# Flamingo layer on one core: TensorE takes over additions of tile 12 and of three outputs, and the slots are reordered

## What is computed

```python
x = x + tanh(g_xattn[0]) * xattn(layernorm(x), ctx, ctx, Wq, Wk, Wv, Wo)   # 16 heads of 64, causal
x = x + tanh(g_ffn[0]) * ffn(layernorm(x), ...)

def ffn(x, ...):
    h = rmsnorm(x, gamma1)
    q = (h @ Wq + bq).reshape(b, t, 16, 8)
    kv = ((h @ Wdown + bdown) @ Wup + bup).reshape(b, t, 16, 16)
    k, v = split(kv)
    att = softmax(einsum('bthd,btgd->bthg', q, k) / sqrt(8))       # heads of one row attend to each other
    x = x + einsum('bthg,btgd->bthd', att, v).reshape(b, t, 128) @ Wo + bo
    h2 = rmsnorm(x, gamma2)
    gate = softmax(h2 @ Wg + bg)                                   # 8 experts
    return x + einsum('btd,edf,bte->btf', h2, We, gate)
```

## Time and profile before

| | us |
|---|---|
| median of 3 runs | 265.44 |
| lowest, highest | 265.3, 267.71 |
| the profiled execution | 265.66 |
| its span | 263.8 |
| PE, DVE, ACT, POOL busy | 236.0, 195.0, 168.3, 159.0 |

### The profile page before, as it was taken

One profiled execution on the slowest core, in us unless ns is written; L12 is line 12 of the kernel. 1 busy time (PEld: TensorE's weight loads), 2 busy tenths in 40 slices (PEclk: granted clock), 3 DMA queues, 4 the chain that ended last, 5 costly groups with the idle time before them and its releaser, 6 DMA issues.

```text
span 263.8 us, 7717 instructions
## 1 busy us (share of the span) xinstructions
PE 236.0 (89%) x3154; PEld 167.0 (63%) x3154; DVE 195.0 (74%) x335; ACT 168.3 (64%) x498; POOL 159.0 (60%) x169
## 2 busy tenths in 40 slices
PE   5989989898999999998999999989999988851781
PEld 3765778586768585857676776867685665530360
DVE  0236644198989796979798832989897999999925
ACT  2437634756686868785877778667868767651452
POOL 4104041619196877878587376691968778739644
PEclk9999999999999999999999999999999999995698
DMA  6990000000000000000000000000000000000000
GB/s 212 369 307 6 2 4 0 6 0 2 0 5 10 2 14 0 4 10 5 11 2 12 2 10 4 10 5 0 2 12 2 11 4 14 0 0 0 12 10 20
DMA packets 6016, 7.28 MB, mean 28 GB/s; under 512 B 477, under 2 KB 4830, under 8 KB 5982
## 3 DMA queue, kind: packets, MB, share of 16 engines
q1 hardware_dynamic: 5550, 6.16, 7.2%
q10 hardware_dynamic: 432, 0.64, 0.7%
HBM read 5.88 MB, written 0.92 MB: 26 GB/s over the span
## 4 chain that ended last, share of the span: by engine, by line
PE 77%; ACT 9%; DVE 7%; issue 3%; DMA 1%; POOL 0%; SPq 0%; DVEq 0%; ACTq 0%; POOLq 0%
PE ps_a L825 47%; PE ps_c L825 11%; PE ps_b L825 9%; PE ps_e L825 5%; PE ps_b L877 3%; ACT exb L462 2%; DVE ps_e L616 2%; DMA cT<-in_ctx_t 1%; ACT probs L407 1%; ACT probsT L414 1%; ACT v_sb L396 1%; DVE psums L583 1%; PE ps_c L921 1%; DVE exb L684 1%; ACT aT L401 1%
## 5 line engine op out<-in xcount | busy, mean ns | idle before, releaser
L268 POOL TENSOR_TENSOR probs<-probs,prinv 120x672 f32<-120x672 f32 x16 | 24.3, 1517 | 48.3 <-DVE prinv L587 48.2
L277 POOL TENSOR_TENSOR prod<-fqkv 128x1280 f32<-128x1280 f32 (+1 forms) x14 | 38.5, 2752 | 1.9 <-DVE fqkv L601 0.7
L825 PE MATMUL ps_a<-aT,wo_sb 128*128 128x112 f32 x256 | 32.9, 281 | 2.1 <-ACT aT L401 1.3
L825 PEld LDWEIGHTS ps_a<-aT,wo_sb 128*128 128x128 f32 x256 | 29.9, 191 | 4.2 <-ACT aT L401 2.0
L644 DVE TENSOR_REDUCE ps_e<-prod 128x128 f32<-128x2048 f32 x14 | 31.9, 2281 | 0.4 <-POOL prod L288 0.4
L616 DVE TENSOR_REDUCE ps_e<-prod 128x256 f32<-128x2048 f32 x14 | 32.0, 2284 | 0.0
L825 PE MATMUL ps_a<-wv_sb,cT 128*64 128x512 f32 x128 | 31.4, 606 | 0.0
L825 PE MATMUL ps_a<-cT,wk_sb 128*128 128x224 f32 x128 | 28.9, 379 | 1.3 <-DMA cT<-in_ctx_t 1.3
L401 ACT COPY aT<-ps_a 128x448 f32<-128x448 f32 x32 | 15.5, 536 | 20.4 <-PE ps_a L825 20.4
L825 PEld LDWEIGHTS ps_a<-cT,wk_sb 128*128 128x128 f32 x128 | 24.6, 203 | 5.6 <-DMA cT<-in_ctx_t 2.9
L825 PE MATMUL ps_a<-xT,wqc 128*128 128x224 f32 x128 | 27.0, 359 | 0.6 <-ACT qT L390 0.6
(11 more groups left out here) (136 smaller groups left out, 468.9 us busy)
## 6 DMA issues: line engine op xcount, KB each, us to landing
xp_sb<-in_xp SPq DMA_DIRECT2D x1, 896.0 KB, 7.8
out<-out_sb SPq DMA_DIRECT2D x14, 64.0 KB, 1.5
xT<-in_x_t SPq DMA_DIRECT2D x1, 784.0 KB, 9.1
cT<-in_ctx_t SPq DMA_DIRECT2D x1, 784.0 KB, 10.6
wv_sb<-in_wv SPq DMA_DIRECT2D x1, 512.0 KB, 7.7
...
```

The lines of the kernel that those rows point to most:

```text
L268: nc.gpsimd.tensor_tensor(pr[0:TG, NC:C, :, 0:S], pr[0:TG, NC:C, :, 0:S], prinv[p % 2][0:TG, NC:C, :].unsqueeze(3).to_broadcast([TG, C - N ...
L277: nc.gpsimd.tensor_tensor(prod1[:, 0:hp, :, :], t[:, D:2 * D].rearrange("p (g d) -> p g d", g=FH).unsqueeze(1).to_broadcast([128, hp, FH, ...
L825: return nc.tensor.matmul(o, lhsT, rhs, start=start, stop=stop, skip_group_check=True)
```

## The change

For tile 12 (PE_SUMS) the products are written with the summed index outermost (prod1 as d, h, g; prod2 as g, h, d), and TensorE adds them: logit_sums with 8 matmuls of 256 columns and head_sums with 16 of 128, the identity as weights, accumulated in ps_e. For the tiles 10, 11 and 12 (PE_OUT) output_sums adds the ten terms with ten matmuls of 128 columns instead of GpSimd's outputs; ScalarE's late_out copies the sum, and SyncE waits for that copy. Tile 13's exponentiated gate lies in PSUM. stay_warm is gone. In the main loop (steps 2 to 13) TensorE does first(fa) behind turn_probs and gate_logits, shift before bias_o, and attend before both expert halves; ScalarE does x1_copy behind turned_probs; GpSimd does weighted before first_scale; VectorE does weighted before gate_logits and scaled_qkv behind head_sums. Steps 14 and 15 and the part after the loop are reordered on all engines.

```diff
 LATE = 10
 HP_LATE = 8
 HQ_LATE = 5
+PE_SUMS = (12,)
+PE_OUT = (10, 11, 12)
 BIG = {11: "b", 12: "a", 13: "b"}
-STAY_WARM = 10
 PROJECT_AT = {t: [("qk"[t % 2], t // 2 + 1, n) for n in range(4)] for t in range(2, NP - 2)}
 
...
 
         def expert_banks(f):
             return {"a": ps_a, "b": ps_b}[BIG[f]] if f in BIG else ps_c
+
+        prod1_d = prod1[:, :, :, :].rearrange("p a b c -> p (a b c)").rearrange("p (d h g) -> p d h g", d=FD, h=FH)
+        prod2_g = prod2[:, :, :, :].rearrange("p a b c -> p (a b c)").rearrange("p (g h d) -> p g h d", g=FH, h=FH)
...
+
+        def logit_products(f, lo, hi, k, q):
+            if f in PE_SUMS:
+                return (prod1_d[:, :, lo:hi, :],
+                        k.rearrange("p (g d) -> p d g", g=FH).unsqueeze(2).to_broadcast([128, FD, n, FH]),
+                        q.rearrange("p (h d) -> p d h", h=n).unsqueeze(3).to_broadcast([128, FD, n, FH]))
+            return (prod1[:, lo:hi, :, :],
+                    k.rearrange("p (g d) -> p g d", g=FH).unsqueeze(1).to_broadcast([128, n, FH, FD]),
+                    q.rearrange("p (h d) -> p h d", h=n).unsqueeze(2).to_broadcast([128, n, FH, FD]))
+
+        def head_products(f, lo, hi, v):
+            n = hi - lo
+            if f in PE_SUMS:
+                return (prod2_g[:, :, lo:hi, :],
+                        e_sb[f % 2][:, lo:hi, :].rearrange("p h g -> p g h").unsqueeze(3).to_broadcast([128, FH, n, FD]),
+                        v.rearrange("p (d g) -> p g d", d=FD).unsqueeze(2).to_broadcast([128, FH, n, FD]))
+            return (prod2[:, lo:hi, :, :],
+                    e_sb[f % 2][:, lo:hi, :].unsqueeze(2).to_broadcast([128, n, FD, FH]),
+                    v.rearrange("p (d g) -> p d g", d=FD).unsqueeze(1).to_broadcast([128, n, FD, FH]))
+
+        def gate_exp(f):
+            return ps_c[:, 1, 256 + E:256 + 2 * E] if f == NT - 1 else gexp[f % 2][:, :]
+
+        def out_sum(f):
+            return ps_a[:, 1, 0:D] if f == PE_OUT[0] else ps_e[:, 0, 0:D]
 
...
             for f in range(NT):
                 if f == NT - 1:
                     sp.wait_ge(s["last_out"], 1)
+                elif f in PE_OUT:
+                    sp.wait_ge(s["late_out"], f - PE_OUT[0] + 1)
                 else:
                     sp.wait_ge(s["out_ready"], f + 1)
                 sp.dma_start(out[f * 128:(f + 1) * 128, :], out_sb[f % 2][:, :]).then_inc(stored[f % 2], 16)
...
+                o, k, q = logit_products(f, 0, hp, t[:, D:2 * D], t[:, 0:hp * FD])
+                nc.gpsimd.tensor_tensor(o, k, q, ALU.mult).then_inc(s["prod1_pool"], 1)
...
+                o, e, v = head_products(f, 0, hq, fqkv[f % 2][:, 2 * D:3 * D])
+                nc.gpsimd.tensor_tensor(o, e, v, ALU.mult).then_inc(s["prod2_pool"], 1)
...
                 if fc is not None:
                     second_scale(fc)
+                if fb is not None:
+                    weighted(fb)
                 if fa is not None:
                     first_scale(fa)
-                if fb is not None:
-                    weighted(fb)
                 if fc is not None:
                     gating(fc)
...
             last, prior, third = NT - 1, NT - 2, NT - 3
             products(prior)
             first_scale(last)
+            products(last)
             weighted(prior)
-            products(last)
             second_scale(third)
-            outputs(third - 1)
+            weighted(last)
             gating(third)
-            weighted(last)
             second_scale(prior)
-            outputs(third)
+            last_residual(last)
             gating(prior)
             second_scale(last)
-            last_residual(last)
-            outputs(prior)
...
-                nc.scalar.activation(gexp[f % 2][:, :], glog[f % 2][:, :], ACT.Exp, bias=gmax[f % 2][:, :],
+                nc.scalar.activation(gate_exp(f), glog[f % 2][:, :], ACT.Exp, bias=gmax[f % 2][:, :],
                                      accum_out=gsum[f % 2][:, :]).then_inc(s["gexp_ready"], 1)
...
+
+            def late_out(f):
+                act.wait_ge(s["out_summed"], f - PE_OUT[0] + 1)
+                act.wait_ge(stored[f % 2], 16 * (f // 2))
+                nc.scalar.copy(out_sb[f % 2][:, :], out_sum(f)).then_inc(s["late_out"], 1)
...
@@ -499,23 +527,24 @@
                 if fc is not None:
                     squares(fc)
                     x2_copy(fc)
-                if fa is not None:
-                    x1_copy(fa)
                 if fb is not None:
                     head_exps(fb)
                 if t < NP:
                     values(t, 0)
                     values(t, 1)
                     turned_probs(t)
+                if fa is not None:
+                    x1_copy(fa)
                 if fc is not None:
                     gate_exps(fc)
                 if t < NP:
                     attended(t, 0)
                     attended(t, 1)
+                if fc is not None:
+                    experts(fc, 0)
                 if fa is not None:
                     kv_copy(fa)
                 if fc is not None:
-                    experts(fc, 0)
                     experts(fc, 1)
...
                 x2_copy(fc)
+                values(t, 0)
                 squares(fc)
                 x1_copy(fa)
+                values(t, 1)
                 turned_probs(t)
-                values(t, 0)
+                gate_exps(fc)
                 head_exps(fb)
-                values(t, 1)
-                gate_exps(fc)
                 attended(t, 0)
                 attended(t, 1)
                 kv_copy(fa)
...
             last, prior, third = NT - 1, NT - 2, NT - 3
+            x1_copy(last)
             o_copy(third)
-            x1_copy(last)
             head_exps(prior)
+            kv_copy(last)
+            squares(third)
             x2_copy(third)
-            squares(third)
-            kv_copy(last)
+            head_exps(last)
+            late_out(PE_OUT[0])
+            o_copy(prior)
             gate_exps(third)
-            o_copy(prior)
-            head_exps(last)
+            x2_copy(prior)
             squares(prior)
             experts(third, 1)
+            o_copy(last)
             experts(third, 0)
-            x2_copy(prior)
             gate_exps(prior)
-            o_copy(last)
+            squares(last)
+            x2_copy(last)
             experts(prior, 1)
-            x2_copy(last)
-            squares(last)
             experts(prior, 0)
             gate_exps(last)
+            late_out(third)
             experts(last, 0)
+            late_out(prior)
...
+                o, k, q = logit_products(f, hp, FH, ps_e[:, f % 2, 2 * D:3 * D], fqkv[f % 2][:, hp * FD:D])
+                if f - 1 in PE_SUMS:
+                    dve.wait_ge(s["logit_ready"], f)
+                nc.vector.tensor_tensor(o, k, q, ALU.mult).then_inc(s["prod1_ready"], 1)
...
+                if f - 1 in PE_SUMS:
+                    dve.wait_ge(s["oraw_ready"], f)
+                o, e, v = head_products(f, hq, FH, ps_e[:, f % 2, 3 * D:4 * D])
+                nc.vector.tensor_tensor(o, e, v, ALU.mult).then_inc(s["prod2_ready"], 1)
...
-                nc.vector.tensor_scalar(gate[f % 2][:, :], gexp[f % 2][:, :], ginv[f % 2][:, :], r2[f % 2][:, :],
+                nc.vector.tensor_scalar(gate[f % 2][:, :], gate_exp(f), ginv[f % 2][:, :], r2[f % 2][:, :],
                                         ALU.mult, ALU.mult).then_inc(s["gate_ready"], 1)
...
@@ -755,17 +785,17 @@
                     norm(t)
                 if fb is not None:
                     shifted_logits(fb)
+                    weighted(fb)
                 if fc is not None:
                     gate_logits(fc)
                 if fb is not None:
-                    weighted(fb)
-                    head_scales(fb)
+                    head_sums(fb)
                 if fc is not None:
                     gate_sum(fc)
                 if fa is not None:
                     scaled_qkv(fa)
                 if fb is not None:
-                    head_sums(fb)
+                    head_scales(fb)
                     normed_heads(fb)
...
+                gate_sum(fc)
                 weighted(fb)
                 head_scales(fb)
-                gate_sum(fc)
                 head_sums(fb)
...
             last, prior, third = NT - 1, NT - 2, NT - 3
+            new_x1(NP - 1)
             products(prior)
-            new_x1(NP - 1)
-            logits(prior)
+            scaled_qkv(last)
+            shifted_logits(prior)
             new_x2(third)
-            shifted_logits(prior)
-            scaled_qkv(last)
             weighted(prior)
             products(last)
-            head_sums(prior)
             head_scales(prior)
+            logits(last)
+            shifted_logits(last)
             gate_logits(third)
             normed_heads(prior)
-            logits(last)
+            weighted(last)
+            new_x2(prior)
+            head_scales(last)
             gate_sum(third)
```

(92 more changed lines are left out.)

24 lines of the change are left out of this document (3 added, 21 removed).

## The result

Each kernel ran 20 times. The changed kernel took 264.75 us in the median (264.07 to 265.78), the kernel before 266.40 us (264.72 to 268.81): a ratio of 0.995 with a 95% interval of 0.9931 to 0.9969. The forecast was 266.2 us and 0.3% slower. Ratios leave out runs that are over 1.5% longer than the fastest of the same kernel, medians don't, so a ratio can differ a little from that of two medians. Two things stand out. The median of three runs from which the forecast started (265.44) was 1 us better than the median of twenty. And the runs of before spread over 4.1 us, those of after over 1.7.

What follows compares the result with a forecast made beforehand. TensorE bounds the loop (77% of the span), VectorE and then a latency chain the tail. Loop +1.85, steps 14 and 15 +0.1, tail -1.2 give +0.75 on 265.66 us, as a median 266.2 us; range 262.3 to 268.8.

Steps and rivals of the forecast that it cites:

- the loop chain: Steps 2 to 13: with first late, turn_probs of steps 4 and 12 wait for GpSimd's norm; 1.85 us lost in total.
- Full steps: Attention loop: the chain takes 13.9 us where TensorE needs 14.16, so they stay unchanged, margin 0.25 us.
- rival B: Loop: the 13.9 us chain also binds full steps, seven paying 0.3 us each: +2.1, 268.3 us; chance 0.16.
- Rival A: Loop chain slack, waits of steps 2, 3 and 11 gone, last DMA not delayed: 262.5 us; chance 0.28.
- The tail: After the loop: 3 us won at x2, half given back by sums and ScalarE's queue; -1.2 us, bounds -3 to 0.
- The delay by the DMA in front: Last output on SyncE: output_sums(12)'s DMA goes first, the last tile's follows 0.47 us behind, at 260.6.
- Steps 14 and 15: VectorE bounds them and its order hardly changes, one gate_sum of 0.1 us moved ahead: +0.1 us.
- The baseline: Whole kernel: +0.75 on the profiled 265.66 us gives 266.4; the median lies 0.22 below, so 266.2 us.
- rival C: TensorE's clock: logit_sums runs at the low level after idling from 231.0 to 232.3: +3.5, 269.7 us; chance 0.08.
- Those named for being right: TensorE idle before turn_probs(4)/(12) ~1 us; steps 5-8 14.2 us; VectorE idle 2-3 us; clock 1.00; gate below 0.3 us.
- sign of being wrong: scores(13) no later than 189.7 us, or the last tile's x2 over 4 us earlier, counted from scores(13).
- The rule that was weighed: GpSimd's strided products: reads with a step over 8 bytes cost about half again; no extra taken, else tail -0.9.

Runs made afterwards that it cites:

- tail_only: The changed kernel with the old order in steps 2 to 13: 263.56 us, ratio 0.9912 to the kernel before.
- no_warm: The kernel before with stay_warm taken out and nothing else: 265.38 us, ratio 0.9933.
- warm_hole: The kernel before with 40 unread identity matmuls in TensorE's hole from 237 to 243 us: 268.81 us, ratio 1.0089.
- before_again: The kernel before, unchanged, run and profiled once more: 266.84 us, ratio 1.0032 to itself.
- dve_sums: The changed kernel with both sums of tile 12 back on VectorE: 266.94 us, ratio 1.0018 to the kernel before.
- mixed: The changed kernel with the new order only in steps 4 to 8, 12 and 13: 263.05 us, ratio 0.9864 to the kernel before.
- best1: The changed kernel with the old loop order, tile 11's output back on GpSimd, gate_exps before expert terms: 262.66 us, ratio 0.9839 to the kernel before.
- best2: As best1, with the new order in steps 5 to 8 and 13: 262.21 us, ratio 0.9816 to the kernel before.

## Why the prediction was wrong

**The loop: mechanism right, size 0.8 us off.** The prediction had the loop chain late at turn_probs of steps 4 and 12, and it is, released by GpSimd's norm, 0.78 and 0.77 us. Up to scores(5) it had 1.2 us lost; the profiles show 1.64 (start to start from scores(2): 40.51 against 38.87), since already step 3 waits, 1.53 us, where the prediction left turn_probs(3) at 60.65; counted from scores(2) it is at 61.05. For steps 11 and 12 it had 0.65, and they show 0.66. Full steps were to be unchanged with a margin of 0.25 us, and none waits: rival B, that the chain binds in all of them, is out. Rival A, a slack chain, is out by the same waits. Two terms were missing. Step 9 lost 0.52, mostly a wait of 0.56 us for the turned probabilities, which ScalarE handed over late. And in the profile of before steps 6 and 8 were 1.17 us longer than in tail_only, the same order without those issue gaps (14.74 and 15.05 against 14.46 and 14.16), and step 2 was 0.27 shorter: 165.05 against 164.15 us from scores(2) to scores(14). In all six profiles with the new order in steps 5 to 8 these take 14.10 to 14.12 us. So the loop cost 1.07 us in the profiles (166.12 against 165.05) where 1.85 was forecast (the prediction's own two times for scores(13) differ by 1.82); against a loop without gaps it cost 1.97. The long steps stood in the trace of before, and I took one step of 14.16 us for all. Why the gaps come and go isn't settled: of eight profiles with the old order in the full steps, five have them at the same two places, and tail_only, no_warm and warm_hole don't.

**The tail: 1.2 us forecast, 2.3 measured. This is the term that turned the sign in the profiles.** All in times less 1.82 us. VectorE's part came out nearly as laid out: new_x1(15) done at 231.8 (forecast 232.2), heads of tile 13 at 249.98 (250.5), x2 at 251.60 (251.85), sums of 3.72 and 3.81 us (3.5 and 3.7). The step that failed comes behind x2, at output_sums(11) in front of gate_logits(13). The sums were put behind turn_x2 at 252.75 and were to end at 255.4, with the gate's logits at 255.95. Measured, turn_x2 was followed by the sums at 252.02, TensorE was free of them for gate_logits at 254.25, and the logits were done at 254.80, 1.15 us early. The lead lasted to the end: the last output was put at 260.05 and ended at 259.08, where it had been 261.75 before. The delay by the DMA in front, put at 0.5 us, was 0.35. So the span ends 2.3 us earlier than before, where 1.2 was forecast.

**Steps 14 and 15.** Forecast +0.1; step 14 took 0.17 us more (12.13 against 11.96).

**The start.** scores(2) began 0.58 us later in after (39.35 against 38.77), before the first moved instruction of the loop. Other runs of one kernel differ by as much (39.48 in the second profile of before); that is scatter.

These together in the profiles: 0.58 + 1.07 + 0.17 - 2.32 = -0.5 us in the span, where +0.75 was forecast.

**The baseline: what the medians add.** I carried the sum from the profiled execution to the median of three runs with -0.22 us. The kernel before is 266.4 over 20 runs, 0.96 above that median and 0.74 above its profile. The missing piece may not be chance alone. The profile showed the clock at 0.50 from 238 us, and I used it only in rival C, against the change. That the same dip was a risk of the kernel before, which reaches stay_warm in some runs and makes 4.42 us of 2.48, I didn't price, though removing exactly these matmuls was part of the change. Of stay_warm I counted only its place in the queue; by itself its removal is worth 1.8 us in the medians, of which the profiles show 1.06 in the tail. But a longer dip also costs the kernel without stay_warm 2.5 us (264.24 to 266.78), so the doubled matmuls can't be its whole price, and how much of the 0.74 us they make is open. In the profiles the change is -0.39 us (265.66 to 265.27), in the medians -1.65: of the difference 0.74 is before's profile lying under its median, 0.52 after's lying above.

**The signs.** Those named for being right all came: TensorE idle before turn_probs of steps 4 and 12 (0.78 and 0.77 us), steps 5 to 8 at 14.11, VectorE idle 2.17 us, the clock at 1.00, the gate in 0.28 us; neither sign of being wrong did. They looked at the loop and at the tail up to x2, and not at the stretch behind x2 or at the baseline, where the forecast failed.

**What is shown and what isn't.** Shown by single edits: the loop order costs (1.0 to 1.2 us on the new tail), the sums of tile 12 bring 1.8 to 2.2 us, the removal of stay_warm some 1.8 (interval 0.8 to 2.8 us), and the gate from PSUM ends its wait but brings no time that can be told. The profiles, cut at the same places, say where (us; the first row from the span's start to scores(2), the last from scores(15) to the span's end):

| | before | before_again | no_warm | tail_only | after | dve_sums |
|---|---|---|---|---|---|---|
| start | 38.77 | 39.48 | 38.73 | 39.53 | 39.35 | 38.91 |
| steps 2 to 13 | 165.05 | 164.78 | 164.15 | 164.15 | 166.12 | 166.12 |
| step 14 | 11.96 | 11.97 | 11.96 | 12.13 | 12.13 | 12.13 |
| the rest | 48.02 | 51.27 | 46.96 | 45.69 | 45.70 | 47.54 |

Not shown: that the held clock itself brings something. For it speaks that every kernel with the clock at 0.999 or more spreads by 1.3 to 1.8 us (after, tail_only, mixed, best1, best2), and every one in which it falls by 2.1 or more; but a spread of 4 runs isn't that of 20. Against a simple form of it speak the two kernels that filled the hole and gained nothing, one of them with the clock at 1.00 in its profile.

**The rule that was weighed.** GpSimd's strided products of tile 12 took 2.54 us (1024 elements) and 1.73 us (640), against 2.37 and 1.53 for the same shapes of tile 13 in the same trace: 7% and 13% more. The Trainium skill, GPSIMD Engine Reference, "Performance pitfalls for Q7 kernels", has a kernel that reads with a step over 8 bytes pay about half as much again per element. The measurement decides, and for these products the rule isn't borne out; taking no extra for it was closer.
